# The LayerNorm statistics ahead of a mixture-of-experts MLP, taken for eight token tiles at once instead of one by one

## What is computed

```python
def _layernorm(x, axis=-1, eps=1e-5):
    m = jnp.mean(x, axis=axis, keepdims=True)
    v = jnp.var(x, axis=axis, keepdims=True)
    return (x - m) / jnp.sqrt(v + eps)

x = x + attn(_layernorm(x))
# E = 8 experts, D = 1024, F = 4096
h = _layernorm(x)
router_probs = softmax(h @ Wr)
expert_idx = argmax(router_probs);  p_max = max(router_probs)
outs[e] = gelu(h @ W1[e] + b1[e]) @ W2[e] + b2[e]      # for every e
x = x + p_max * outs[expert_idx]
```

## Time and profile before

| | before |
|---|---|
| median of 3 runs | 11390.93 us |
| the 3 runs | 11390.93, 11316.49, 12827.68 us |
| time of the profiled execution | 11314.03 us |
| its span, slowest core (core 2) | 11312.5 us |
| spans of the 8 cores | 11269.8 to 11312.5 us |
| span of the second slowest core (core 4) | 11291.3 us |
| PE busy | 8936.1 us (79%) |
| ACT busy | 2219.1 us (20%) |
| DVE busy | 1805.0 us (16%) |

### The profile page before, as it was taken

How to read it: one execution, slowest core, us unless ns; L and a number is a source line. 1 busy time by engine, 2 the same in 40 slices (tenths; PEclk the granted TensorE clock), 3 DMA queues, 4 the chain that set the end, 5 groups by cost and what they waited for, 6 DMA issues and landing times.

```text
span 11312.5 us, 114005 instructions; the slowest of 8 cores (11269.8 to 11312.5 us)
## 1 busy us (share of the span) xinstructions
PE 8936.1 (79%) x43561; PEld 4153.5 (37%) x44384; DVE 1805.0 (16%) x3027; ACT 2219.1 (20%) x3276; POOL 1377.2 (12%) x2414
## 2 busy tenths in 40 slices
PE   3444447999999999999834544389999999999998
PEld 1222223444444444444312222234444444444443
DVE  2344442000000000000024444410000000000000
ACT  1222212122111122111112222121222111221111
POOL 0000001111111111111100000011111111111111
PEclk7665658999999999999956556589999999999999
DMA  9999602333333333333320000023333334333333
GB/s 140 110 110 110 69 8 66 113 97 101 103 112 108 121 101 105 104 108 112 117 52 1 1 1 1 8 68 111 97 101 98 113 107 126 97 101 103 112 107 115
DMA packets 262992, 999.46 MB, mean 88 GB/s; under 512 B 44832, under 2 KB 45088, under 8 KB 258352
## 3 DMA queue, kind: packets, MB, share of 16 engines
q0 software_dynamic: 254176, 958.56, 35.8%
q1 hardware_dynamic: 8288, 33.55, 0.9%
HBM read 1128.14 MB, written 150.99 MB: 113 GB/s over the span
## 4 chain that ended last, share of the span: by engine, by line
PE 74%; DVE 12%; ACT 6%; issue 5%; another core or an unknown queue 2%; DMA 1%; DVEq 1%; ACTq 0%; POOL 0%; POOLq 0%
PE p_ov L60 26%; PE p_st L60 24%; DVE arena L60 9%; PE p_x L60 9%; PE p_ok L60 6%; PE p_tp L60 5%; ACT arena L60 5%; PE p_a L60 5%; DVE x_buf L60 3%; ACT L60 1%; DMA arena<-w2sc 1%; DVEq L72 1%; ACTq L72 0%; DMA arena<-wr 0%
## 5 line engine op out<-in xcount | busy, mean ns | idle before, releaser
L60 PE MATMUL p_ov<-arena 128*128 128x512 bf16 (+1 forms) x13526 | 3433.1, 388 | 323.4 <-DVE x_buf L60 179.2
L60 PE MATMUL p_st<-arena 128*128 128x512 bf16 (+2 forms) x13054 | 3154.4, 372 | 38.9 <-DVE x_buf L60 22.1
L60 PEld LDWEIGHTS p_ov<-arena 128*128 128x128 bf16 (+1 forms) x13824 | 1385.7, 105 | 1994.5 <-issue 635.7
L60 PEld LDWEIGHTS p_st<-arena 128*128 128x128 bf16 (+1 forms) x13312 | 1256.3, 100 | 1566.6 <-issue 152.2
L60 ACT ACTIVATE arena<-p_ov,arena 128x512 bf16<-128x512 f32 x1024 | 703.5, 687 | 4671.2 <-PE p_ov L60 4623.4
L60 POOL DMA_DIRECT2D arena<-w2sc x2048 | 1099.4, 537 | 3506.6 <-PE p_tp L60 3505.0
L60 PE MATMUL p_x<-arena 128*128 128x512 bf16 (+2 forms) x4251 | 1373.1, 407 | 112.8 <-ACT arena L60 75.9
L60 DVE SCALAR_TENSOR_TENSOR x_buf<-p_ov,arena,x_buf 128x512 f32<-128x512 f32 x128 | 96.0, 750 | 7050.8 <-PE p_tp L60 7043.8
L60 PE MATMUL p_ok<-arena 128*128 128x512 bf16 (+3 forms) x3584 | 1015.1, 331 | 18.3 <-DVE x_buf L60 9.0
L60 PE MATMUL p_a<-arena 128*128 128x512 bf16 (+2 forms) x3002 | 844.2, 336 | 91.5 <-DVE arena L60 82.6
L60 ACT ACTIVATE arena<-p_st,arena 128x512 bf16<-128x512 f32 x1024 | 703.5, 687 | 1041.8 <-PE p_st L60 992.2
(11 more groups left out here) (84 smaller groups left out, 2452.3 us busy)
## 6 DMA issues: line engine op xcount, KB each, us to landing
arena<-w2sc POOLq DMA_DIRECT2D x2048, 256.0 KB, 2.9
arena<-w1sc POOLq DMA_DIRECT2D x256, 1024.0 KB, 6.1
w1sc<-w POOLq DMA_DIRECT2D x8, 8192.0 KB, 410.4
w2sc<-w POOLq DMA_DIRECT2D x8, 8192.0 KB, 1021.6
x_buf<-x SPq DMA_DIRECT2D x2, 8192.0 KB, 45.2
y<-x_buf SPq DMA_DIRECT2D x4, 4096.0 KB, 12.4
arena<-wq POOLq DMA_DIRECT2D x2, 2048.0 KB, 30.8
arena<-wk POOLq DMA_DIRECT2D x2, 2048.0 KB, 46.8
```

Source lines behind the costliest of these rows:

```text
L60: ins = getattr(e, fname)(*args, **kw)
```

## The change

`ln2_parts` now returns ten functions. A new first one, `stats_all`, takes the statistics of all 8 tiles of the group: per tile the row sum, the negated mean into column `tl` of `f_rt`, the square of `x` itself, and the sum of the squares. Three instructions on 8 columns turn these into variances (the mean of the squares less the square of the mean), and one Ln and one Exp on ACT give all 8 reciprocal standard deviations. A tile is then only the apply, one DVE instruction with two per-partition operands that reads `x_buf` directly, the 8 transposes, and the copy. The centred copy `f_lnc` is no longer written. `router` is as before (only its indentation differs).

```diff
--- before.py
+++ after.py
@@ -762,77 +762,91 @@
             g0 = grp * (GRP // 128)
             l4 = [0]
             l5 = [0]
+            rstd_act = [0]
+
+            def stats_all():
+                for tl in range(8):
+                    xt = x_buf[:, (g0 + tl) * D:(g0 + tl + 1) * D]
+                    P.wait(v, "pe", l4[0])
+                    P.op(v, "tensor_reduce", f_sm[:, 0:1], xt, axis=AX.X, op=ALU.add)
+                    P.op(v, "tensor_scalar", f_rt[:, tl:tl + 1], f_sm[:, 0:1],
+                         -1.0 / D, None, ALU.mult)
+                    P.op(v, "tensor_tensor", f_xns, xt, xt, ALU.mult)
+                    P.op(v, "tensor_reduce", f_rt[:, 8 + tl:9 + tl], f_xns,
+                         axis=AX.X, op=ALU.add)
+                P.op(v, "tensor_scalar", f_rt[:, 8:16], f_rt[:, 8:16], 1.0 / D, None,
+                     ALU.mult)
+                P.op(v, "tensor_tensor", f_rt[:, 16:24], f_rt[:, 0:8], f_rt[:, 0:8],
+                     ALU.mult)
+                st = P.op(v, "tensor_sub", f_rt[:, 8:16], f_rt[:, 8:16],
+                          f_rt[:, 16:24], inc="dve")
+                P.wait(a, "dve", st)
+                P.op(a, "activation", f_rt[:, 16:24], f_rt[:, 8:16], AF.Ln,
+                     bias=c_eps[:])
+                rstd_act[0] = P.op(a, "activation", f_rt[:, 16:24], f_rt[:, 16:24],
+                                   AF.Exp, scale=-0.5, inc="act")
 
             def tile(tl):
-              def f():
-                  TT = g0 + tl
-                  xt = x_buf[:, TT * D:(TT + 1) * D]
-                  P.wait(v, "pe", l4[0])
-                  P.op(v, "tensor_reduce", f_sm[:, 0:1], xt, axis=AX.X, op=ALU.add)
-                  P.op(v, "tensor_scalar", f_sm[:, 1:2], f_sm[:, 0:1], -1.0 / D, None,
-                       ALU.mult)
-                  P.op(v, "tensor_scalar", f_lnc[:], xt, f_sm[:, 1:2], None, ALU.add)
-                  P.op(v, "tensor_tensor", f_xns, f_lnc[:], f_lnc[:], ALU.mult)
-                  l1 = P.op(v, "tensor_reduce", f_sm[:, 2:3], f_xns, axis=AX.X,
-                            op=ALU.add, inc="dve")
-                  P.wait(a, "dve", l1)
-                  P.op(a, "activation", f_sm[:, 3:4], f_sm[:, 2:3], AF.Ln,
-                       bias=c_eps[:], scale=1.0 / D)
-                  l2 = P.op(a, "activation", f_sm[:, 4:5], f_sm[:, 3:4], AF.Exp,
-                            scale=-0.5, inc="act")
-                  P.wait(v, "act", l2)
-                  l3 = P.op(v, "tensor_scalar", f_xns, f_lnc[:], f_sm[:, 4:5], None,
-                            ALU.mult, inc="dve")
-                  P.wait(t, "dve", l3)
-                  P.wait(t, bank_free[7][0], bank_free[7][1])
-                  for dt in range(8):
-                      l4[0] = P.op(t, "transpose", p_tp[:, dt * 128:(dt + 1) * 128],
-                                   f_xns[:, dt * 128:(dt + 1) * 128], id128[:],
-                                   inc="pe" if dt == 7 else None)
-                  P.wait(a, "pe", l4[0])
-                  l5[0] = P.op(a, "activation",
-                            gx[:, 0:8192].rearrange("p (dt tk) -> p dt tk", tk=GRP)
-                            [:, :, tl * 128:tl * 128 + 128],
-                            p_tp[:, 0:1024].rearrange("p (dt tk) -> p dt tk", tk=128),
-                            AF.Copy, inc="act")
-                  bank_free[7] = ("act", l5[0])
-              return f
+                def f():
+                    xt = x_buf[:, (g0 + tl) * D:(g0 + tl + 1) * D]
+                    P.wait(v, "act", rstd_act[0])
+                    P.wait(v, "pe", l4[0])
+                    l3 = P.op(v, "tensor_scalar", f_xns, xt, f_rt[:, tl:tl + 1],
+                              f_rt[:, 16 + tl:17 + tl], ALU.add, op1=ALU.mult,
+                              inc="dve")
+                    P.wait(t, "dve", l3)
+                    P.wait(t, bank_free[7][0], bank_free[7][1])
+                    for dt in range(8):
+                        l4[0] = P.op(t, "transpose", p_tp[:, dt * 128:(dt + 1) * 128],
+                                     f_xns[:, dt * 128:(dt + 1) * 128], id128[:],
+                                     inc="pe" if dt == 7 else None)
+                    P.wait(a, "pe", l4[0])
+                    l5[0] = P.op(a, "activation",
+                                 gx[:, 0:8192].rearrange("p (dt tk) -> p dt tk",
+                                                         tk=GRP)
+                                 [:, :, tl * 128:tl * 128 + 128],
+                                 p_tp[:, 0:1024].rearrange("p (dt tk) -> p dt tk",
+                                                           tk=128),
+                                 AF.Copy, inc="act")
+                    bank_free[7] = ("act", l5[0])
+                return f
 
             def router():
...
-            return [tile(i) for i in range(8)] + [router]
...
+            return [stats_all] + [tile(i) for i in range(8)] + [router]
```

More of the change, by code:

```diff
@@ L801, in router @@
-            def router():
[L802 to L833, removed]
@@ new lines, in router @@
+            def router():
+                P.wait(t, "act", l5[0])
+                P.wait(t, bank_free[6][0], bank_free[6][1])
+                for tl in range(8):
+                    for dt in range(8):
+                        r1 = P.op(t, "matmul", p_x[:, tl * 8:tl * 8 + 8],
+                                  gx[:, dt * GRP + tl * 128:
+                                     dt * GRP + tl * 128 + 128],
+                                  f_wr[:, dt * 8:(dt + 1) * 8],
+                                  start=(dt == 0), stop=(dt == 7),
+                                  inc="pe" if (tl == 7 and dt == 7) else None)
+                P.wait(v, "pe", r1)
+                L3 = p_x[:, 0:64].rearrange("p (tt e) -> p tt e", e=8)
+                P.op(v, "tensor_reduce", f_sm[:, 8:16], L3, axis=AX.X, op=ALU.max,
+                     negate=True)
+                r2 = P.op(v, "tensor_tensor",
+                          f_rt[:, 0:64].rearrange("p (tt e) -> p tt e", e=8), L3,
+                          f_sm[:, 8:16].unsqueeze(2).broadcast_to([128, 8, 8]),
+                          ALU.add, inc="dve")
+                bank_free[6] = ("dve", r2)
+                P.wait(a, "dve", r2)
+                r3 = P.op(a, "activation", f_rt[:, 64:128], f_rt[:, 0:64], AF.Exp,
+                          inc="act")
+                P.wait(v, "act", r3)
+                P.op(v, "tensor_reduce", f_sm[:, 8:16],
+                     f_rt[:, 64:128].rearrange("p (tt e) -> p tt e", e=8), axis=AX.X,
+                     op=ALU.add)
+                P.op(v, "reciprocal", f_sm[:, 0:8], f_sm[:, 8:16])
+                P.op(v, "tensor_scalar", f_rt[:, 64:128], f_rt[:, 0:64], 0.0, None,
+                     ALU.is_equal)
+                P.op(v, "tensor_tensor", gw[:].rearrange("p (tt e) -> p tt e", e=8),
+                     f_rt[:, 64:128].rearrange("p (tt e) -> p tt e", e=8),
+                     f_sm[:, 0:8].unsqueeze(2).broadcast_to([128, 8, 8]), ALU.mult,
+                     inc="dve")
```

## The result

The changed kernel takes 11247.91 us in the median of 9 runs, 11206.18 us in the fastest. Against the kernel before, measured beside it again in 10 runs, the ratio is 0.9869 with a 95% interval of 0.9811 to 0.9926: faster, by less than 2%. The profiled execution took 11207.70 us where that of before took 11314.03, 106.3 us less. The ratio leaves out executions in which a whole die ran at a lower granted clock, but it can still hold ones in which two neighbouring cores did so for a while. Much of what follows is about those.

A forecast was written before the change was run, and what follows sets the result against it. Experts' matmuls fill most of the span, so gains come only where LayerNorm stops the PE. Savings of 22.0 + 60.0 + 2.2 - 1.0 = 83.2 us from 11314.0 give 11231 us, range 11190 to 11330.

The forecast's parts named there:

- the two parts of the sum: Group 0's exposed statistics, 22.0 us saved in all, and group 1's tiles inside expert 0, 60.0 us saved.
- the restart at MM2: First eight matmuls of MM2 no longer begin right after idle time: 1.1 us per batch goes, 2.2 us in all.
- tile 7: Group 1's last tile, now in expert 1, adds 0.5 us per batch, -1.0 us in the sum.
- rival 1: Denser expert 0 brings on more stretches at 0.81 clock, 28 us each; 11345 us with four beyond break-even; chance 0.05.
- The sum below is made against 11314.03: Base of the forecast: the profiled execution's 11314.03 us, from which the saved 83.2 us were taken.
- The range: Likeliest 11211 to 11248 us; one stretch fewer or more gives 11190 to 11276, upper end taken to 11330.
- The DVE pass: Statistics of all 8 tiles on DVE: 34.8 us, with the square from `x_buf` taken at 1.22 us.
- Group 0: From DVE's first row to the router's matmuls: 55.3 us against 66.3, saving 11.0 us per batch.
- The new wait: Expert 0, before block 6: PE stalls about 20 us for a GELU that ACT holds behind group 1's Ln.
- After the stall: Rest of expert 0: 26 blocks 89.8 us, restart 1.5, transposes 3.5, last GELU wait 1.9; 138.8 us together to MM2.
- The table switch: ACT: 28 table loads fewer; a drain per switch, by the skill page, would cost 2.8 us more per batch, 11236 us.
- Rivals 2 to 4: 2: group 1's gain lost, 11292 us, 0.07; 3: no ACT stall, 11191 us, 0.04; 4: W1 loads bound, 11310 us, 0.03.

The follow-up runs named there:

- e1: Changed kernel with the new statistics for group 0 only, group 1 back in the tile-by-tile form; profiled execution 11427.7 us, none clean.
- e2: Changed kernel with the new statistics for group 1 only, group 0 back in the tile-by-tile form; 11228.9 us in its profiled, clean execution.
- e3: Changed kernel with the second reduction of each tile of the DVE pass written twice; execution of 11280.6 us, none clean.
- e8: The same kernel as e6, measured again; 11111.6 and 11113.1 us in two clean executions, ratio 0.9807 to the kernel before.
- e6: e5 with a second buffer and PSUM bank for odd tiles of group 0; group 0's part 29.7 to 30.3 us, no clean execution.
- e4: Changed kernel with group 1's Ln and Exp moved from after step 0 to after step 2 of expert 0; 11162.8 us, clean.
- e5: Changed kernel with the DVE pass written in BN_STATS and BN_AGGR; 11128.4 us in a clean execution, ratio 0.9853 to the kernel before.

## Why the prediction was right or wrong

The mechanism was right: the two parts of the sum came nearly as forecast. On core 2, whose rows the forecast used, they fell by 83.8 us against 84.2 in the sum (22.0 + 60.0 + 2.2, the restart at MM2 with them and tile 7 not). From clean execution to clean execution the kernel gained 87 us (ratio 0.9923) against 83.2. The time of 11247.91 us lies inside the range, and the change is less than 2%, as given a chance of 0.95. What was wrong is the level and the size as measured: the clean executions lie at 11204 to 11210 us and not at 11231, the ratio is 0.9869 where 11231 / 11314 = 0.9927 lies just outside its interval, and the profiled executions differ by 106.3 us and not 83.2. That 11231 is only 17 us from the median of 11247.91 is luck: that median is an execution in which cores 6 and 7 stood above the rest, at 11217.5 and 11246.4 us.

- **The step that failed: "The sum below is made against 11314.03".** That execution held, by the prediction's own rival 1, 28 us of a low granted clock on core 2 that belong to no step of the kernel; core 2's tail was 24 to 31 us longer than that of cores 0, 1 and 4 to 7. The text priced them, put them into the range, and left them in the base of the sum. Carried through, the base is the second slowest core's 11291.3 us plus 1.5, and the forecast 11210 us; the changed kernel's clean executions are 11204 to 11210. The ratio has a raised base too. It is the mean of 11207.70, 11206.18, 11207.88, 11206.45 and 11247.91 us over that of 11313.49, 11316.49, 11390.93 and 11437.22 us, and all four of the kernel before lie 20 to 143 us over its clean level. The spans of the cores in those four are not on record, so that a pair at a low clock is likely there but not shown. Whether the change makes such stretches rarer or this was chance stays open. The runs beside the experiments give no sign that it does: without the executions that a ratio leaves out, five of six there were clean for the kernel before, and six of seven in all for the changed one. Such stretches were met in e1, e2, e3 and e8 too.
- **The range:** 11211 less 28 us is 11183, not the 11190 that the text gives; and a kernel slower by 2% than the one before would need about eleven stretches of 28 us, not more than eight, since the 83 us saved come first. Neither changes the reading.
- **The DVE pass:** 34.6 us for 34.8; the square straight from `x_buf` took 1.23 us like the one of `f_lnc`. Right.
- **Group 0:** 55.2 us for 55.3, with a loop of 2.33 us. The apply with two operands took 0.81 us, between the 0.75 taken and the bound of 1.22, and hidden. Right; but the loop hangs on the one `f_xns` as closely as on the one `p_tp` (e6), which the text did not see.
- **The new wait:** a stall of 20.00 us on core 1 and 19.1 to 20.2 on all, forecast at about 20, released by ACT. Right in place, size and cause (e3, e4). The first GELUs of step 1 were done at 42.5 us; the text says 42.1, while its own terms (39.1 + 1.3 + 1.5) give 41.9.
- **After the stall** the first block took 6.24 us against 3.62 on core 1, 2.6 us more and not 1.5. Over the cores and batches it was 1.5 to 2.9 us more, so that the bound of 2.0 was too tight. Transposes took 0.44 us (0.5), the last of them partly beside the wait for the last GELU: 1.32 us of idling remained, not 1.9. Together 139.7 us for 138.8.
- **The table switch:** 28 loads fewer, as forecast. The Trainium skill's drain of about 1380 ns behind each load (ScalarE: Activation LUTs, "What ACT_TABLE_LOAD costs") is not in this trace: Ln starts at 1754.59, 0.02 us after the load's end, and the load back starts at 1755.26, 0.07 us after Exp's end, and is followed by a GELU at 1756.56.
- **Rival 1** names stretches that are real, with a cause that the runs don't bear out: the low granted clock comes to neighbouring cores two at a time, without the change too, and e1's and e8's stretches lie in the last experts, not where expert 0 has become denser. Rivals 2 to 4 fell: full rate came back within one block, the stall was there, and the PE's rows of expert 0 show no wait for a load of W1.

## What to carry to other kernels

Before a sum is made against one profiled execution, compare its cores: where one or two of them stand 20 us over the rest with a lower granted clock, the base is that of the others, and the difference of two such executions says nothing to 0.3%. Batching small statistics takes them out of a tile-by-tile chain. But where an engine runs its stream in order, the one batched instruction must stand in it where its input is done: here moving Ln and Exp two steps on was worth another 44 us. After that, ask what the batch itself costs. This pass lies on the PE's path in four places: a microsecond more of it cost about 4 us (e3), and a pass shorter by 18.9 us gave back 79 us (e5). A loop through single buffers may hang on two of them at once; give both a second before you judge.

## What the runs showed of the hardware

- A BN_STATS over 128x512 fp32 took 694 ns and a BN_AGGR of two of them 209 ns, so that mean and variance of 1024 elements cost 1.90 us where row sum, square and row sum took 4.23.
- A granted clock of about 0.8 of full came on pairs of neighbouring cores alone (0 and 1 in e1, 2 and 3 in the kernel before and in e8, 6 and 7 in e3), for a loss of some 28 us up to some 155 us. No run shows what starts such a stretch.
- Function-table loads took 1283 ns each in all kernels (76 of them in the changed one), also directly before a GELU.
- First blocks after little work or idling cost 1.0 us (core 2, kernel before, block 0 of batch 0) to 2.9 us (core 4, changed kernel, after the stall) more than a block in the run, and not a fixed amount for nearly the same idle time: after the stalls of 19.3 to 20.2 us in batch 0 of the changed kernel it was 1.5 to 2.9 us on its eight cores.
